# Where the head products stand among the jobs of a half-step: single groups beside jobs, or two groups in units of their own

## The reference

```python
h = h + attn(_layernorm(h))
h = h + ffn(_layernorm(h))
# attn
qkv = x @ qkv_weight.T                     # split into 12 heads of 16
q = _layer_norm(q) * SCALE
k = _layer_norm(k)
attn = softmax(einsum('bhnd,bhmd->bhnm', q, k))
out = einsum('bhnm,bhmd->bhnd', attn, v)   # then @ proj_weight.T
# ffn
x1 = clip(gelu(xq @ wq1.T * alpha_w1 * a1 + b1), -10, 10)
x2 = hq @ wq2.T * alpha_w2 * a2 + b2       # xq, hq rounded to -8..7
```

## Time and profile before

| | |
|---|---|
| median of 3 runs | 1069.84 us (1069.6 to 1072.44) |
| span of the profiled execution | 1067.6 us |
| PE busy | 979.4 us, 92% |
| ACT busy | 872.6 us, 82% |
| DVE busy | 813.9 us, 76% |
| groups of heads (L1247) | 394.7 us of PE |
| scores (L1227) | 264.3 us of PE |
| exponentials (L682) | 736.1 us of ACT |

### The profile page before, as it was taken

One profiled execution on the slowest core, in us unless ns is written; L12 is line 12 of the kernel. 1 busy time (PEld: TensorE's weight loads), 2 busy tenths in 40 slices (PEclk: granted clock), 3 DMA queues, 4 the chain that ended last, 5 costly groups with the idle time before them and its releaser, 6 DMA issues.

```text
span 1067.6 us, 19577 instructions
## 1 busy us (share of the span) xinstructions
PE 979.4 (92%) x7571; PEld 389.1 (36%) x7571; DVE 813.9 (76%) x2325; ACT 872.6 (82%) x950; POOL 411.8 (39%) x345
## 2 busy tenths in 40 slices
PE   5589999999999999999999999999999999989885
PEld 4333433334342433434343343434334343413223
DVE  5878869788686969878696977869697886825347
ACT  1387788897979889797988979798888989798883
POOL 6555513635343353534435363443526412201000
PEclk9899999999999999999999999999999999999997
DMA  7511200303011040202102040110202000000000
GB/s 162 127 16 16 31 1 2 46 1 64 12 25 22 1 75 1 38 8 58 18 2 45 1 73 3 31 16 16 30 1 45 1 16 1 16 1 1 16 1 31
DMA packets 25762, 28.62 MB, mean 27 GB/s; under 512 B 5027, under 2 KB 22182, under 8 KB 25670
## 3 DMA queue, kind: packets, MB, share of 16 engines
q0 software_dynamic: 16896, 11.80, 9.4%
q1 hardware_dynamic: 8624, 15.55, 4.8%
q10 hardware_dynamic: 150, 0.01, 0.0%
HBM read 21.06 MB, written 6.29 MB: 26 GB/s over the span
## 4 chain that ended last, share of the span: by engine, by line
PE 40%; ACT 30%; DVE 24%; issue 3%; POOL 3%; DMA 0%
ACT probs L682 22%; PE ps_o L1247 12%; PE ps_s L1227 8%; PE ps_j L1271 4%; ACT gelu L676 4%; PE ps_j L1279 3%; PE ps_j L1325 3%; POOL stack L592 3%; PE ps_j L1286 2%; PE ps_j L1292 2%; ACT L676 2%; ACT L682 2%; DVE hn L797 2%; PE ps_j L1311 2%; PE ps_j L1296 2%
## 5 line engine op out<-in xcount | busy, mean ns | idle before, releaser
L682 ACT ACTIVATE probs<-ps_s 128x1024 f32<-128x1024 f32 x768 | 736.1, 1023 | 125.5 <-PE ps_s L1227 120.6
L1247 PE MATMUL ps_o<-probs,v_sb 128*32 128x512 f32 x3072 | 394.7, 605 | 0.2 <-DVE o_sb L859 0.2
L1227 PE MATMUL ps_s<-qT,kT 64*128 64x512 f16 x1536 | 264.3, 384 | 35.0 <-ACT probs L682 25.2
L592 POOL TENSOR_TENSOR stack<-sq,stack 128x384 f16<-128x384 f32 x124 | 120.5, 992 | 162.9 <-DVE stack L846 162.9
L1227 PEld LDWEIGHTS ps_s<-qT,kT 64*128 64x128 f16 x1536 | 61.5, 93 | 299.5 <-ACT probs L682 267.6
L525 POOL DMA_INDIRECT h_all<-in_L_tok_token_table,idx x60 | 96.7, 1611 | 59.5 <-DMA h_all<-in_L_tok_segm_table,idx 41.2
L1247 PEld LDWEIGHTS ps_o<-probs,v_sb 128*32 128x32 f32 x3072 | 69.1, 109 | 124.3 <-issue 116.1
L601 POOL TENSOR_TENSOR y_sb<-y_sb,b_row 128x768 f32<-128x768 f32 x14 | 25.4, 1814 | 198.8 <-DVE y_sb L931 198.8
L581 POOL TENSOR_TENSOR sq<-qk 128x384 f32<-128x384 f32 x56 | 46.2, 826 | 139.5 <-DVE qk L894 139.5
L525 POOL DMA_INDIRECT h_all<-in_L_tok_segm_table,idx x56 | 87.2, 1557 | 15.2 <-issue 13.1
L1279 PE MATMUL ps_j<-wh,partsT 128*128 128x384 f16 (+1 forms) x384 | 71.5, 296 | 1.0 <-ACT partsT L663 0.7
(11 more groups left out here) (201 smaller groups left out, 1118.5 us busy)
## 6 DMA issues: line engine op xcount, KB each, us to landing
out<-h_all SPq DMA_DIRECT2D x15, 384.0 KB
h_all<-in_positions SPq DMA_DIRECT2D x7, 768.0 KB
gelu<-in_L_ffn_w SPq DMA_DIRECT2D x2, 576.0 KB
h_all<-in_L_tok_token_table,idx POOLq DMA_INDIRECT x60
h_all<-in_L_tok_segm_table,idx POOLq DMA_INDIRECT x56
probs<-in_L_attn_qkv_weight SPq DMA_DIRECT2D x2, 432.0 KB, 4.7
h_all<-in_positions SPq DMA_DIRECT2D x2, 384.0 KB, 8.0
o_nat<-in_L_ffn_alpha_a SPq DMA_DIRECT2D x1, 384.0 KB
```

The source lines that it names most:

```text
L592: last = nc.gpsimd.tensor_tensor(low, src, high, ALU.subtract)
L682: nc.scalar.activation(probs[:, u % PROBS, 2 * pair:2 * pair + 2], ps_s[:, 2 * pair:2 * pair + 2], ACT.Exp, scale=SCORE_SCALE).then_inc(ex ...
L1227: last = mm(ps_s[:, j], kT[rows, par, head // 2, m * P:(m + 1) * P], qT[rows, par, head // 2, nh * NQ:(nh + 1) * NQ], start=True, stop=True)
L1247: last = mm(ps_o[32 * j:32 * j + 2 * D, :], v_sb[:, par, m, (GH * group + j) * VE:(GH * group + j) * VE + 2 * D], probs[:, u % PROBS, j], ...
```

## The change

Nineteen lines of `PLAN` are written anew, in two stretches: units 5 to 12, and units 15 to 23. Before, nearly each of these units holds one `h`, mostly beside jobs. Now units with two `h` and at most one job alternate with units that hold jobs and no `h`, or nothing for PE at all. The jobs keep their order among one another, and so their banks. On DVE `x1` goes ahead of `D2`, and `E3` behind `x3` and `x4`. Lines 0 to 4, 13 and 14 are as they were.

```diff
-h l0 h R0
-W3 m0 h
-W4 h
-h N0 W5 I0
-I1 h o A0
-I2 h A1 A2
-h A3 I3
-C0 B0 X0
+h h l0 R0
+W3 m0
+h h W4
+N0 W5 I0 I1
+h h o
+A0 I2 A1 A2
+h h A3
+I3 C0 B0 X0
...
-h S0 n0
-h n1 o
+S0 n0
+h h n1 o
 D0 x0 E0 C1
-n2 h C2 D1
-E1 n3 h
-D2 h x1
-h D3 E2 x2
-E3 x3 x4 h
-x5 C3 h
+n2 h h
+C2 D1 E1 n3
+h h x1
+D2 D3 E2 x2
+h h x3 x4
+E3 x5 C3
```

## The result

The changed kernel takes 1124.01 us (median of 4 runs, 1122.46 to 1126.37) against 1069.89 for the kernel before: 1.050 times as long, 95% interval 1.048 to 1.052. The profiled execution's span grew from 1067.6 to 1120.7, by 53.1 us. The forecast was 47.6 more for both, 1117.4 us: the measured time lies 6.6 above it, 1 us over the forecast's 1112 to 1123 and inside the outer range, 1104 to 1128.

What follows compares the result with a forecast made beforehand. PE was taken to bound units with many jobs, ACT those with one group of heads and little else. Losses of 30.8 + 11.2 + 5.6 = 47.6 us on 1069.84 gave 1117.4 us, range 1112 to 1123 (60%), outer 1104 to 1128.

Steps and rivals of the forecast that it cites:

- cycles in half-steps 1 to 13: Units 5 to 14 lose 1.40 us, units 14 to 23 with unit 0 lose 0.97; 2.37 a half-step, 13 times, 30.8.
- half-steps 14 and 15: Without jobs A to E, ACT bounds both stretches; the change loses 2.1 + 3.5 = 5.6 us, twice, 11.2.
- wait for the copy of `E3`, 7 times: Unit 0's first scores wait for DVE's later copy: 0.8 us in the 7 even half-steps 2 to 14, 5.6 us.
- The cycle: A unit without heads plus one with two groups takes 4.60 us, where two ACT-bound units took 3.88.
- One sign: In the changed trace, the second pair of scores of each unit with two groups waits for an exponential.
- Jobs under the light unit: In units without heads, 1.62 us of PE time is free; the moved jobs fit and cost nothing.
- Rival 1: PE is the bound throughout, so fewer mode changes gain 1.56 us a half-step, 23 us: 1046 us; 4%.
- Rivals 2 and 6: 2: gain and loss meet, 1070 us, 2%. 6: slack in units 0 to 4 or 13 halves the loss, 1094, 6%.
- Rival 3: The same loss at half-step starts and cycles but without the `E3` wait: 1111.8 us; 15%.
- Rival 4: DVE falls 1.5 us further back and bounds units 14 to 23, about 14 us more: 1131 us; 10%.
- Rival 5: PE's clock falls in half-steps 14 and 15, where PE idles more, 34 us more: 1151 us; 3%.

Runs made afterwards that it cites:

- the short exponentials: Exponentials of 64 of 512 columns only, read eight times over: 1042.88 us with the plan before, 1064.91 with the changed plan, 1053.26 with that plan and E3 copied earlier.

## Why the prediction was right

The mechanism held, and the sum came out 5.5 us short. The sum's terms against the changed kernel's trace, from the starts of the half-steps:

| term | forecast | measured |
|---|---|---|
| cycles in half-steps 1 to 13 | 30.8 | 32.3 |
| half-steps 14 and 15 | 11.2 | 11.4 |
| wait for the copy of `E3`, 7 times | 5.6 | 7.6 |
| half clock once, in unit 0 of half-step 10 | no term | 1.6 |
| start of the kernel | 0 | 0.2 |
| together | 47.6 | 53.1 |

*The cycle.* Forecast 4.60 from the earlier trace rows, measured 4.60. Units 5 to 12 with the Gelu unit lose 1.4 to 1.5 a half-step, 1.9 in half-step 13 (forecast 1.40), units 14 to 23 with unit 0 1.02 where no `E3` is waited for (forecast 0.97). One sign failed: not every double unit's second pair waits, as unit 22 shows. The even half-steps took 63.7 us, the odd ones 65.5: the forecast had named 64.0 for odd and 64.8 for even ones, since it counted the wait for `E3` in the half-step behind the wait, and the starts of the exponentials count it in the one ahead.

*Jobs under the light unit.* They fitted. The one wait of some size there, 0.43 for POOL in unit 21 of the changed kernel, went over the free time a little: units 21 and 22 took 4.63 together.

*Half-steps 14 and 15.* Twelve exponentials in 13.80 us, where the earlier trace rows has 11.70 (start and length of the stretch, then PE, PEld, DVE, ACT, POOL):

```profile
977.40:991.20 13.80, 10.11 (x80) 2.61 (x78) 5.41 (x20) 11.32 (x12) 0.00 (x0) 1.00 0.00 0
```

That the two half-steps together came so close is in part luck, since unit 13 wasn't in the sum. Before, each of the two had a stretch at half clock there (granted 0.50 and 0.51). In the changed kernel half-step 14 had none and its unit 13 was 1.3 us shorter, while the stretch in half-step 15 (0.51) was longer, and its unit 13 by 1.1 us.

*The copy of `E3`* is the term that was mis-sized. PE waited 1.83 us (571.64 above), forecast 1.5, and it cost 1.1 at each start of an even half-step where I had 0.8. VectorE was later than summed by 0.3: x1 took 2.58 us in place of 2.36, as two of its three instructions ran beside POOL's work and took twice their time (L879 and L880 take 0.49 and 0.43 in x3):

```profile
562.68 0.54 DVE L878 TENSOR_SCALAR gelu<-gelu,ia,qlo 128x512 f32<-128x512 f32 x1
563.26 1.02 DVE L879 TENSOR_SCALAR gelu<-gelu,qhi 128x512 f32<-128x512 f32 x1
564.31 1.02 DVE L880 TENSOR_SCALAR hq<-gelu 128x512 bf16<-128x512 f32 x1
```

```profile
562.84 2.21 POOL L592 TENSOR_TENSOR stack<-sq,stack 128x384 f16<-128x384 f32 x2 [1.46 <-DVE stack L846]
```

*The rivals.* Rival 1 (faster, TensorE the bound) fell by the waits for ACT; the short exponentials show that even without ACT its 23 us don't come, since VectorE and POOL then bound the same units. Rivals 2 and 6 (no loss, or half of it) fell because nothing was made up: from unit 1 to unit 6 half-step 7 took 13.78 us in both kernels. Rival 3 (no wait for `E3`) fell by the 1.83 us. Rival 4 (VectorE the bound of units 14 to 23) needed VectorE 1.5 us later than summed; it was 0.3 later, and in half-steps 1 to 13 of the trace no job `Y` waits for an `x`. Rival 5 named the right mechanism in the wrong place. The clock stayed at 1.00 in the light and double units of half-steps 14 and 15, but fell once in half-step 10, behind the wait for `E3`:

```profile
696.00:700.00 4.00, 3.02 (x31) 1.09 (x23) 3.79 (x9) 3.48 (x4) 0.00 (x0) 1.00 0.00 0
700.00:704.00 4.00, 3.16 (x16) 0.74 (x20) 2.43 (x6) 1.94 (x2) 0.00 (x0) 0.63 0.00 0
```

The price, 1.6 us for one double unit of the profiled execution, was missing from the sum as a term of that wait.

## What to carry to other kernels

Where two engines hand buffers to and fro with no spare one, the sum of work over a stretch doesn't tell its time: each unit has to be paid by itself. A unit shorter than the partner's time gives nothing to the next, and a long one behind it is late from its start; so spread the work evenly, and look for a unit of the new kind in the old trace before writing a plan of them. The gain from putting like products together (0.12 us for each change of mode here) is worth having only where the engine isn't waiting for anyone.

## What was not expected of the hardware

Behind two light units in a row TensorE's clock fell to the 1.2 GHz level in each of half-steps 2 to 14 (granted 0.51 behind a stretch of 5.5 us with 3.74 busy), though no single wait in them was longer than 0.91 us, and some 0.8 us of added work, an estimate from four jobs `I` at 0.21, took 15 us off the kernel. Behind one light unit between double ones, as in units 6 to 9 of the changed kernel, it didn't fall: 3.07 to 3.46 us busy in 4.50 and a clock of 1.00. The kernel's time thus isn't a smooth function of the plan: the same bunching costs 54 us in one order and 77 in another.
